# One graph layer on a Trainium2 core: the order of the first stage's matrix products

## The reference, cut to what matters

```python
def adjacent_mat(adj):
    adj = adj + jnp.eye(adj.shape[0], dtype=adj.dtype)
    deg = jnp.sum(adj, axis=1)
    dinv = jnp.where(deg > 0, deg ** (-0.5), 0.0).astype(adj.dtype)
    return dinv[:, None] * adj * dinv[None, :]

def reference(x, adj):                 # x: 1354 x 512, adj: 1354 x 1354, float32
    h = jnp.maximum(_layernorm(x, axis=-1), 0.0)
    y = adj @ adjacent_mat((adj + adj.T) * 0.5)
    y = y @ h
    return x + y
```

## Time and profile before

| | us |
|---|---|
| median of three runs | 181.61 |
| lowest and highest of the three | 181.34 and 183.07 |
| the profiled execution, its own time | 181.94 |
| its span, first to last instruction | 180.2 |
| TensorE busy | 164.4 |

### The profile page before, as it was taken

How to read it: one execution, slowest core, us unless ns; L and a number is a source line. 1 busy time by engine, 2 the same in 40 slices (tenths; PEclk the granted TensorE clock), 3 DMA queues, 4 the chain that set the end, 5 groups by cost and what they waited for, 6 DMA issues and landing times.

```text
span 180.2 us, 1916 instructions
## 1 busy us (share of the span) xinstructions
PE 164.4 (91%) x704; PEld 131.0 (73%) x704; DVE 85.4 (47%) x140; ACT 77.1 (43%) x134; POOL 29.1 (16%) x55
## 2 busy tenths in 40 slices
PE   0029999999999999999999999999999999999992
PEld 0027888888888888886788888888888888888760
DVE  0457767888885974965054134251331513401101
ACT  4468879898995983914324023031130320100000
POOL 1125955345324610000000000000000000000000
PEclk9999999999999999999999999999999999999999
DMA  6999999988996000000013942010110101101001
GB/s 180 352 407 412 408 412 384 337 325 322 310 302 159 4 0 0 0 0 0 4 34 85 395 161 88 28 62 0 58 58 0 58 4 58 58 0 58 22 36 34
DMA packets 8745, 25.29 MB, mean 140 GB/s; under 512 B 877, under 2 KB 1133, under 8 KB 8737
## 3 DMA queue, kind: packets, MB, share of 16 engines
q1 hardware_dynamic: 8737, 25.18, 38.9%
HBM read 22.26 MB, written 2.77 MB: 139 GB/s over the span
## 4 chain that ended last, share of the span: by engine, by line
PE 91%; DMA 3%; DVE 2%; SPq 1%; ACT 1%; issue 0%
PE bank L482 91%; DMA S<-in_adj_dram 3%; SPq L164 1%; DVE ring L385 1%; ACT ring L283 1%; SPq L165 0%; ACT g L294 0%; DVE y_out L436 0%; DVE S L352 0%; SPq L160 0%; DVE g_scale L380 0%; DVE d_scale L376 0%
## 5 line engine op out<-in xcount | busy, mean ns | idle before, releaser
L482 PE MATMUL bank<-g,ring 128*128 128x512 f32 (+1 forms) x352 | 83.8, 402 | 12.2 <-ACT g L294 12.2
L482 PEld LDWEIGHTS bank<-g,ring 128*128 128x128 f32 (+1 forms) x352 | 66.3, 189 | 29.3 <-issue 12.2
L482 PE MATMUL bank<-z,ring 128*128 128x512 f32 (+1 forms) x352 | 80.8, 391 | 0.0
L482 PEld LDWEIGHTS bank<-z,ring 128*128 128x128 f32 (+1 forms) x352 | 64.7, 184 | 15.9
L301 ACT CAST ring<-AT 128x1408 fp32r<-128x1408 f32 (+1 forms) x11 | 14.6, 1324 | 47.1 <-PE bank L482 47.1
L436 DVE TENSOR_TENSOR y_out<-bank,x_res 128x512 f32<-128x512 f32 (+1 forms) x11 | 7.6, 692 | 52.1 <-PE bank L482 45.2
L420 DVE TENSOR_TENSOR ring<-AT,ring 128x1280 fp32r<-128x1280 f32 (+1 forms) x11 | 15.8, 1440 | 6.0 <-ACT ring L301 6.0
L363 DVE SCALAR_TENSOR_TENSOR S<-S,AT 128x1354 f32<-128x1354 f32 (+1 forms) x11 | 17.4, 1581 | 0.6 <-POOL S L211 0.4
L385 DVE TENSOR_TENSOR ring<-S,ring 128x1024 fp32r<-128x1024 f32 x10 | 12.3, 1233 | 7.9 <-ACT ring L283 7.9
L306 ACT ACTIVATE z<-bank,d_scale 128x512 fp32r<-128x512 f32 (+1 forms) x12 | 7.4, 693 | 14.5 <-PE bank L482 14.5
L283 ACT CAST ring<-S 128x1024 fp32r<-128x1024 f32 x11 | 11.4, 1035 | 2.5 <-DVE S L352 2.5
(11 more groups left out here) (39 smaller groups left out, 37.5 us busy)
## 6 DMA issues: line engine op xcount, KB each, us to landing
AT<-in_adj_t_dram SPq DMA_DIRECT2D x10, 677.0 KB, 6.2
S<-in_adj_dram SPq DMA_DIRECT2D x10, 677.0 KB, 7.9
x_in<-in_x_dram SPq DMA_DIRECT2D x11, 256.0 KB, 5.1
x_res<-in_x_dram SPq DMA_DIRECT2D x1, 2560.0 KB, 9.7
out_dram<-y_out SPq DMA_DIRECT2D x10, 256.0 KB
AT<-in_adj_t_dram SPq DMA_DIRECT2D x2, 256.0 KB, 3.4
S<-in_adj_dram SPq DMA_DIRECT2D x2, 256.0 KB, 4.4
AT<-in_adj_t_dram SPq DMA_DIRECT2D x1, 507.8 KB, 7.2
```

The source lines that it names most:

```text
L482: return nc.tensor.matmul(dst, stationary, rhs[0:r, parts[1], :], start=first, stop=final)
```

## The change

The change rewrites `step(k)`. For k = 0 nothing moves: eight head-by-head matmuls over the banks, then eight of rest by head, then eight of head by rest, with a wait before each group. For k = 1 to 9 the three matmuls of one bank now stand together, in the order head by head, head by rest, rest by head, and the banks follow one another. The waits for `rests` and `g_ready` stand ahead of the whole step; those for `heads` and `g_head` are left out, since a rest is only made after its head.

```diff
             def step(k):
-                pe.wait_ge(heads, k + 1)
-                pe.wait_ge(g_head, k + 1)
-                for parts in ((0, 0), (1, 0), (0, 1)):
-                    if parts == (1, 0):
-                        pe.wait_ge(rests, k + 1)
-                    if parts == (0, 1):
-                        pe.wait_ge(g_ready, k + 1)
-                    for i in range(LO):
-                        last = product(bank[i][:, :], k, i * P, P, g[:, k], P, parts, k == 0 and parts == (0, 0),
-                                       False)
+                ways = ((0, 0), (1, 0), (0, 1))
+                if k == 0:
+                    order = [(i, parts) for parts in ways for i in range(LO)]
+                    pe.wait_ge(heads, 1)
+                    pe.wait_ge(g_head, 1)
+                else:
+                    order = [(i, parts) for i in range(LO) for parts in ((0, 0), (0, 1), (1, 0))]
+                    pe.wait_ge(rests, k + 1)
+                    pe.wait_ge(g_ready, k + 1)
+                for i, parts in order:
+                    if k == 0 and i == 0 and parts == (1, 0):
+                        pe.wait_ge(rests, 1)
+                    if k == 0 and i == 0 and parts == (0, 1):
+                        pe.wait_ge(g_ready, 1)
+                    last = product(bank[i][:, :], k, i * P, P, g[:, k], P, parts, k == 0 and parts == (0, 0), False)
                 last.then_inc(chunk_used, 1)
```

## The result

The changed kernel takes 181.93 us (median of 20 runs, 181.50 to 182.46), the kernel before 181.17 us (20 runs, 180.23 to 183.07). The ratio is 1.0038, with a 95% interval from 1.0020 to 1.0057: a small loss, but clear of zero, 0.69 us by the ratio (the two medians lie 0.76 us apart). The forecast was 181.8 us, in a range from 181.1 to 182.9; the time lies in the range. But the first three runs of the kernel before had a median of 181.61, and 20 runs put it 0.44 us lower: the forecast of +0.22 us was too small by half a microsecond. That 181.8 came so near to 181.93 is luck: a baseline that was too high made up for a loss that was put too low.

A forecast was written before the change was run, and what follows sets the result against it. TensorE's row of matmuls was taken to bound the kernel: 0.76 us of waiting less 0.54 us gained by pace gave +0.22 us, put on the three-run median of 181.61 us: 181.8 us, range 181.1 to 182.9.

The forecast's parts named there:

- TensorE bounds the kernel, and only pace and lateness count: Whole kernel: TensorE busy 164.4 of 180.2 us; everything else counts only where it makes a matmul late.
- The pace, 230.5 ns instead of 233.3, 0.54 us gained: Steps 2 to 9: the new order saves 2.8 ns on each of 192 matmuls, 0.54 us.
- the forecast's own sum: Step 2 starts 0.76 us late, less 0.54 us gained by pace: +0.22 us; without the gain, +0.76 us.
- a sign, 229 to 231.5 ns: New profile: matmul pace expected from the 49th matmul to the tail step; 233 or more would refute the forecast.
- the pace stays: Steps 1 to 9: pace stays 233.3 ns, set by changing stationary blocks; only waits count, +0.76 us, 182.4 us; chance 25%.
- The waits: Ahead of steps 1 and 2: TensorE waits for the rest of g, 0.56 and 0.76 us late; no later stall.
- the restart: After a wait on TensorE: time from operand ready to matmul start, taken as 0.25 us, bounds 0.12 and 0.31.
- That the rest of g[2] comes late because of the masks on GpSimd: VectorE waited until 23.07 us for a GpSimd power, late behind tail masks, diagonal and variance; rest written at 25.83 us.
- The rival of the clock: A stall ahead of step 1 or 2 brings back the lower clock, costing 1.7 us more: 183.5 us; chance 4%.
- The later rest of g: Loads or GpSimd's chain come 1 us later in most runs, moving the end by 1 us: 182.8 us; chance 6%.

The follow-up runs named there:

- e1_same_again: The kernel before, unchanged, profiled a second time; 181.84 us in one run.
- e11_same_third: The kernel before, unchanged, profiled a third time; 180.86 us in one run.
- e2_old_order_new_waits: The kernel before in its old matmul order, with only the change's waits for both rests ahead of each step from step 1 on; 181.73 us, ratio 1.0041.
- e3_new_order_from_3: The kernel before in steps 0 to 2, the new order and its waits from step 3 on; 181.28 us, ratio 1.0007.
- e12_warm_new_order_from_3: The kernel before with 36 small matmuls ahead of step 0 and the new order with its waits from step 3 on; 181.64 us, ratio 1.0004.
- e10_waits_step2_only: The kernel before in its old order, with both rests awaited ahead of step 2 alone; 181.88 us, ratio 1.0024.
- e4_after_masks_late: The changed kernel with GpSimd's tail masks moved behind the powers of row block 5; 181.72 us, ratio 1.0032.
- e8_after_powers_first: The changed kernel with GpSimd's powers of row block b ahead of the diagonal of row block b + 1; 181.49 us, ratio 1.0006.
- e7_after_warm: The changed kernel with 36 small float32 matmuls ahead of step 0; 182.64 us, ratio 1.0057.
- e9_waits_step1_only: The kernel before in its old order, with both rests awaited ahead of step 1 alone; 181.77 us, ratio 1.0008.
- e5_after_rest_g_first: The changed kernel with VectorE's rest of g[n-1] made ahead of the addition of row block n; 185.70 us, ratio 1.0239.

## Why the prediction was right, and where it was not

*TensorE bounds the kernel, and only pace and lateness count:* right. In the profiles of the edits that moved the time beyond their interval, the start of a step of TensorE had moved, or its pace or clock.

*The pace, 230.5 ns instead of 233.3, 0.54 us gained:* the step that failed. The prediction compared two stretches of one execution, and put their difference down to the order. The runs show no such effect: 228.9 ns by kind in `e1_same_again`, `e11_same_third` and behind the stalls of `e2_old_order_new_waits`, 228.9 bank by bank in the changed kernel, both in one execution of `e3_new_order_from_3`, and 233.3 bank by bank in `e12_warm_new_order_from_3`. The order's share of the pace is zero. With the term gone, the forecast's own sum is +0.76 us, and +0.69 was measured. The pace that the prediction had set as a sign, 229 to 231.5 ns, came out (228.9) and proved nothing, since the old order goes at it too. +0.76 us is the number of the rival "the pace stays", but its reason, the change of stationary blocks, has nothing behind it either: the pace did not stay, it was never the order's. The Trainium skill ("TensorE: Matmul & The Clock Gate", section "Wait — 56ns, not 53.3ns?") gives a distance of back-to-back matmuls that has the number of columns in it and not their order. On the order the runs bear it out, and the prediction set it aside too soon; its 215.7 ns for 512 columns no run here shows, nor one single pace for them.

*The waits:* right in place (steps 1 and 2, none later), in what they wait for, in the second containing the first, and in the restart: 0.25 us were taken, and 0.15 + 0.08 = 0.23 us measured. The 0.76 us were near the mean of three profiles and not a constant. The new order pins step 2 to the rest of g[2] plus 0.15 us, and the first matmul behind a restart takes 0.08 us longer than a running one (in `e10_waits_step2_only` and elsewhere 0.31 us from start to start instead of 0.23). The three profiles of the kernel before began step 2 at 0.50, 0.02 and 1.02 us ahead of that rest: with 0.15 and 0.08 us on top, 0.73, 0.25 and 1.25 us to lose, 0.74 in the mean. This is also why the changed kernel has no quick runs: a short slow start is worth something to the old order, which needs the rest of g only 3.7 us into a step, and nothing to the new one.

*That the rest of g[2] comes late because of the masks on GpSimd:* wrong as it stands. `e4_after_masks_late` shows that the masks lie in the wait for the load of row block 3: the diagonal begins 8.51 us after the first matmul with them and 8.55 without. In the earlier trace rows the instructions stand back to back with no wait among them, and the prediction took the filled time for the cause. With the powers ahead of that diagonal (`e8_after_powers_first`) the masks are what they stand behind. So the masks and the load end almost together, and to take one of them away shows only the other.

*The rival of the clock* did not occur in the changed kernel, whose stalls were 0.24 and 0.38 us by the loads' rows; but it is real. Behind a stall of 2.25 us `e7_after_warm` shows the granted clock at 0.50, and half of its runs show no such loss; behind one of 1.32 us in the same execution, ahead of step 0, and one of 0.70 us in `e10_waits_step2_only` the clock stayed at 1.00. What else the fall hangs on was not tried.

*The later rest of g* as a rival of its own was the right mechanism under the wrong heading: counted from the first matmul, the rest of g[2] comes after 13.52 to 13.75 us, while step 0 took from 7.07 to 8.29 us. The first matmul itself starts between 11.50 and 12.85 us, but the rest of g[2] moves with it, in both kernels.

## What to carry to other kernels

A wait moved to the front of a step takes away the slack of every run, and the median shows it less than the spread: when a change narrows the spread by losing the quick runs, look for what the engine is now pinned to. A difference of 2% in pace between two stretches of one trace is no evidence for what differs between them in the code; take a second profile of the same kernel before a sum rests on it. Idle time of an engine with overlapping rows hides in the overlap: read the weight loads, or the distances from start to start.

## What the runs showed of the hardware that was not expected

Matmuls of 128 by 512 ran at one of two steady paces, 228.9 or 233.3 ns from start to start. Of the fourteen profiles, two have 233.3 in most of the steps, one in each order: the first of the kernel before, from the end of its slow start to the tail step, and `e12_warm_new_order_from_3`, from the stall ahead of step 3 to the tail step. Three more have it for one step: `e2_old_order_new_waits` and `e9_waits_step1_only` in step 0 behind the slow start, until the stall ahead of step 1, and `e5_after_rest_g_first` in step 7, between two stalls. So in these traces the pace changed at a stall or at the tail step and not within a running stretch. What chooses between them stays open. The choice is worth 216 x 4.4 ns = 0.95 us in the steps, more than the change.

The first matmuls after 12 us of idleness went at 0.43 us from start to start, for a length that differed from run to run (step 0 took 7.1 to 8.3 us where 5.5 are due); 36 small matmuls ahead of them took this away and made the kernel before 0.7% faster. The profile's clock column reads 1.00 in that stretch, so there only the pace of the rows tells it; in the fall of `e7_after_warm` the column and the pace agree.
